# A two-layer decoder on one core: the last expert stage and the last norm in one stage, hidden rows made transposed

## The chip, the cores and the metric

The kernel runs on one core of one Trainium2 chip. The metric is the device time of one execution in microseconds (us), lower is better; the times before are the median of three runs. A profile comes from one further execution. The engines are TensorE (PE, with its weight loads as PEld), VectorE (DVE), ScalarE (ACT), GpSimd (POOL) and SyncE (SP). SyncE only issues DMAs here. ACTq, SPq and POOLq stand for what these engines' sequencers issue, DMAs above all.

## The reference, cut to what matters

A batch of 32 sequences of 128 tokens with 128 features passes six sublayers; each is followed by a residual add and a layer norm without gain. All is float32. The last two sublayers are a gated recurrence over the 128 positions (`_L1_xattn_ref`) and a switch layer, in which each token goes to one of 8 experts:

```python
logits = t @ switch_w + switch_b
route_prob = jax.nn.softmax(logits, axis=-1)
route_prob_max = jnp.max(route_prob, axis=-1)
routes = jnp.argmax(route_prob, axis=-1)
for e in range(8):
    h = jax.nn.gelu(t @ w1[e] + b1[e])      # w1: 128 x 512
    y = h @ w2[e] + b2[e]                   # w2: 512 x 128
    out = jnp.where((routes == e)[:, None], y, out)
out = out * route_prob_max[:, None]
...
x = _layernorm(x + _L1_ffn_ref(...))
```

## The kernel before

The program is a row of phases. Each is a `Phase`: its engines' programs are written out side by side and joined by semaphores, and at its end stands a barrier over all engines. `phase_encode` does the first layer's attention and cross attention and `phase_experts` (tag `m0`) its experts; `phase_decode` does the second layer's attention, `phase_recurrent` its recurrence, `phase_experts` (tag `m1`) the switch experts, and `phase_finish` the last residual and norm. In every phase the order of work on an engine is written out by hand as ticks: in each tick an engine takes tile n of one step, tile n-2 of another, and so on.

**`phase_recurrent` (L1759).** One tick is one position of the recurrence, for 32 sequences: VectorE multiplies gate and state (`gated`, L2002), TensorE adds the product to `drive` (L1879), ScalarE takes the tanh (L1946), and VectorE waits for it. Beside this chain, four positions make a line of 128 tokens: its output product, its norm (`x6`, the residual of the last sublayer; statistics L2008, GpSimd's power function L1859, scaling L1966) and its routing logits. Four lines make a quad, which VectorE routes at the ticks `quad_at(tick, 29)` to `(tick, 38)`: distance to the largest logit (`gap`), the chosen expert (`hot`), and the rows in the sorted table. GpSimd scatters the line's 128 rows into `scratch_sorted1` (L1850), a table with one region for each expert; SyncE stores the line to `scratch_x6` as well (L1832). `RING` is 12 line buffers. After the last line, VectorE builds the tables (`dve_table`, L427): which expert each of 40 tiles of 128 sorted rows belongs to, and where it begins. SyncE writes a tile of zeros behind each expert's rows (`sp_pads`, L418), ScalarE takes the exponential of all gaps (L1987), and VectorE makes the weights of it.

**`phase_experts` (L1184), tag `m1`.** 40 tiles, which is the most that can be needed; a tick is one tile. SyncE loads a tile of sorted rows (L1230). TensorE transposes it (L1255), ScalarE copies the transpose to SBUF (L1313), TensorE multiplies it with the expert's up weights, which are the moving operand, 512 columns (L1249). VectorE adds the up bias (L1290), ScalarE takes the Gelu (L1326), TensorE transposes the four blocks of 128 hidden columns (L1259), VectorE copies them to SBUF (L1296), TensorE multiplies them with the down weights (L1267), VectorE adds the down bias (L1301) and SyncE stores the tile to `scratch_expert_out1` (L1234). Up and down weights of all experts lie in SBUF, 2 MB each, loaded in `phase_decode` (L1477), and so do the biases, repeated in all partitions.

**`phase_finish` (L2091).** Eight turns of four lines, in a loop with two sets of buffers. SyncE loads four lines of `x6` (L2114), GpSimd gathers each token's expert row with an indirect DMA (L1350), VectorE multiplies with the weight and adds the residual (L2162), takes statistics (L214, L218), GpSimd takes the power function of the variances (L261), VectorE scales (L242) and ScalarE's queue stores the line (L2130).

Of the kernel before, what the change touches and what calls it, by code (L numbers as in the profile page):

```python
# [20 lines left out]
G = 4  # L21
# [11 lines left out]
TILES1 = TOKENS // P + EXPERTS  # L33

# [71 lines left out]
def dram_tile(d, n):  # L106
# [9 lines left out]
    ("a_w1", FF1), ("a_w2", FF1), ("mask_q", G), ("part_iota", 1), ("a_bq", 1), ("a_bk", 1), ("x_bq", 1),  # L116
# [301 lines left out]
def sp_pads(sp, c, t, sorted_rows):  # L418

    sp.wait_ge(t["free_ready"], 1)  # L420
    for e in range(EXPERTS):
        row = sp.value_load(t["free"][0:1, e:e + 1], min_val=0, max_val=EXPERTS * REGION - P)
        sp.dma_start(sorted_rows[bass.ds(row, P), :], c["zeros"][:]).then_inc(t["padded"], 16)
    sp.wait_ge(t["padded"], 16 * EXPERTS)

def dve_table(nc, dve, c, kept, t):  # L427
# [9 lines left out]
    def step(ins):  # L437
# [17 lines left out]
    step(nc.vector.tensor_scalar(tile[:], c["iota_tiles"][:, 0:tiles], last[:], None, ALU.min))  # L455
# [8 lines left out]
                                        op0=ALU.mult, op1=ALU.add))  # L464
    nc.vector.tensor_copy(kept["tile_expert"][:], expert[:])
# [79 lines left out]
def phase_encode(nc, c, d, scr, keep, experts0):  # L545

    with Phase(nc) as ctx:
# [47 lines left out]
        def _(sp):  # L595
# [22 lines left out]
            sp_pads(sp, c, table, scr["sorted0"])  # L618
# [545 lines left out]
def expert_buffers(nc, ctx, tag, down):  # L1164
    def sb(name, shape):
        return ctx.enter_context(nc.sbuf_tensor(name + tag, shape, F32))
    return dict(up=sb("up", [P, EXPERTS, FF1]), up_b=sb("up_b", [P, EXPERTS, FF1]),
                 down=sb("down", [P, EXPERTS, down, P]), down_b=sb("down_b", [P, EXPERTS, P]))

def load_experts(sp, keep, e, d, names, parts=(0, 1, 2, 3)):

    up, down, up_b, down_b = names
    for part in parts:
        tile, src = ((e["up"], d[up]), (e["down"], d[down]), (e["up_b"], d[up_b].partition_broadcast(P)),
                     (e["down_b"], d[down_b].partition_broadcast(P)))[part]
        sp.dma_start(tile[:], src).then_inc(keep["experts_loaded"], 16)
# [238 lines left out]
def phase_decode(nc, c, d, keep, scr, xT_all, experts1, recur):  # L1416
# [4 lines left out]
    with Phase(nc) as ctx:  # L1421
# [45 lines left out]
        def _(sp):  # L1467
# [291 lines left out]
def phase_recurrent(nc, c, scr, keep, e, xT_all):  # L1759
# [5 lines left out]
    with Phase(nc) as ctx:  # L1765
# [19 lines left out]
        x6, x6T = [sb(f"x6_{k}", [P, P]) for k in range(RING)], pair("x6T", [P, P])  # L1785
        stats, mv, ve, rstd, shift = ([sb(f"{n}{k}", [P, w]) for k in range(4)] for n, w in (
            ("stats", 6), ("mean_var", 2), ("var_eps", 1), ("rstd", 1), ("shift", 1)))
        raw, logits, gap = sb("raw", [P, SLOTS, EXPERTS]), sb("logits", [P, SLOTS, EXPERTS]), sb("gap", [P, TILES, EXPERTS])
# [5 lines left out]
        total = sb("total", [P, TILES])  # L1794
# [13 lines left out]
        gaps_ready, weighed = sem("gaps_ready"), sem("weighed")  # L1808
# [276 lines left out]

LINKS6 = 16

def phase_finish(nc, c, keep, scr, out):  # L2091
# [198 lines left out]
```

## Time and profile before

| | |
|---|---|
| median of 3 runs | 1457.57 us (1446.95 to 1458.02) |
| profiled execution | 1453.48 us, span of its trace 1451.7 us |
| busy share of the span | TensorE 83%, VectorE 74%, ScalarE 58%, GpSimd 37% |
| recurrent stage | up to about 1285 us |
| second expert stage | about 1285 to 1383 us |
| finish | about 1385 us to the end |

### The profile page before, as it was taken

To read this page: it belongs to the slowest core of one execution; us is meant where nothing else is said; L and a number is where in the kernel's file an instruction comes from. 1 tells how busy PE (TensorE), PEld (TensorE's weight loads), DVE (VectorE), ACT (ScalarE), POOL (GpSimd) and SP (SyncE) were. 2 spreads that over 40 slices of the span, in tenths; PEclk is the share of its full clock that TensorE was granted. 3 is DMA by queue.
4 is the path that set the end of the run, shared out by engine and by line. 5 is a ranking of instruction groups with operands and counts; after the bars stand their busy time and mean duration, and the time that the engine had idled before them with its cause. 6 is when DMAs were issued, how large, how long until landed. Compare 5 with 4: busy or idle time off the path is not lost. (4 is left out here: it accounts for less than half of the span.)

```text
span 1451.7 us, 31640 instructions
## 1 busy us (share of the span) xinstructions
PE 1207.3 (83%) x9948; PEld 806.1 (56%) x9948; DVE 1076.9 (74%) x3184; ACT 845.2 (58%) x2331; POOL 534.8 (37%) x798
## 2 busy tenths in 40 slices
PE   3889999999999999872999689999997899859900
PEld 2556666666666656541666355555554777637700
DVE  3578888888888888764788599999997466456644
ACT  2678878787878788641566256666665344333300
POOL 1233324344444444424000465655531146510065
PEclk9999999999999999985999799999999599779965
DMA  7100000000000000001222223130000001112133
GB/s 275 28 13 14 16 16 27 20 25 22 23 23 22 22 16 14 14 10 57 69 84 82 58 98 125 40 94 23 22 5 1 6 24 41 36 59 59 50 92 90
DMA packets 84815, 65.88 MB, mean 45 GB/s; under 512 B 11440, under 2 KB 79792, under 8 KB 83760
## 3 DMA queue, kind: packets, MB, share of 16 engines
q1 hardware_dynamic: 73856, 47.18, 10.5%
q0 software_dynamic: 6144, 12.60, 2.6%
q10 hardware_dynamic: 4656, 4.10, 0.9%
q8 instruction: 85, 1.39, 0.4%
q14 instruction: 74, 0.61, 0.1%
HBM read 40.76 MB, written 23.07 MB: 44 GB/s over the span
## 5 line engine op out<-in xcount | busy, mean ns | idle before, releaser
L693 PE MATMUL e_bank_turned<-c_matrices,e_probs 128*128 128x128 f32 x1024 | 165.0, 285 | 17.2 <-ACT e_probs_t L925 9.8
L925 ACT ACTIVATE e_probs_t<-e_bank_turned 128x512 f32<-128x512 f32 x256 | 154.8, 605 | 16.6 <-PE e_bank_turned L693 14.9
L629 POOL TENSOR_TENSOR e_rstd<-e_var_eps,c_minus_half 128x1 f32<-128x1 f32 x128 | 71.1, 576 | 250.6 <-DVE e_var_eps L961 250.3
L1047 DVE TENSOR_REDUCE e_neg_max<-e_bank_scores 128x4 f32<-128x512 f32 x160 | 109.6, 685 | 49.2 <-PE e_bank_scores L736 48.6
L693 PEld LDWEIGHTS e_bank_turned<-c_matrices,e_probs 128*128 128x128 f32 x1024 | 115.9, 144 | 40.8 <-issue 17.0
L703 PE MATMUL e_bank_mix<-e_probs_t,e_values 128*32 128x128 f32 x2048 | 111.5, 291 | 15.7 <-ACT e_probs_t L925 15.4
L884 ACT ACTIVATE e_probs<-e_scores,e_neg_max 128x128 f32<-128x128 f32 x384 | 123.3, 410 | 1.1 <-DVE e_neg_max L1083 1.1
L1249 PE MATMUL m_wide<-up,m_rowsT 128*128 x224 | 119.0, 614 | 0.5 <-ACT m_rowsT L1313 0.4
L1657 ACT ACTIVATE d_probs_t<-d_bank_turned 128x512 f32<-128x512 f32 x128 | 77.3, 604 | 62.7 <-PE d_bank_turned L1542 62.6
L1290 DVE TENSOR_TENSOR m_pre<-m_wide,up_b 128x512 f32<-128x512 f32 x112 | 77.3, 690 | 43.9 <-PE m_wide L1249 42.8
L879 ACT ACTIVATE e_probs<-e_scores 128x512 f32<-128x512 f32 x128 | 82.1, 641 | 42.1 <-DVE e_scores L1080 41.6
L632 POOL TENSOR_TENSOR e_k_by_place<-e_q_k_k,c_matrices 128x512 f32<-128x512 f32 x64 | 66.6, 1040 | 102.4 <-DVE e_q_k_k L1091 102.4
L1641 ACT ACTIVATE d_probs<-d_scores 128x512 f32<-128x512 f32 x128 | 80.8, 631 | 39.5 <-DVE d_scores L1680 39.5
L1542 PE MATMUL d_bank_turned<-c_matrices,d_probs 128*128 128x128 f32 x512 | 81.8, 283 | 21.4 <-ACT d_probs_t L1657 21.3
L1680 DVE TENSOR_TENSOR d_scores<-d_bank_scores,d_neg_max 128x512 f32<-128x512 f32 x128 | 88.5, 692 | 4.4
L1080 DVE TENSOR_TENSOR e_scores<-e_bank_scores,e_neg_max 128x512 f32<-128x512 f32 x128 | 88.3, 690 | 3.4
L1313 ACT ACTIVATE m_rowsT<-m_turned_rows 128x128 f32<-128x128 f32 x112 | 30.9, 276 | 100.3 <-PE m_turned_rows L1255 100.2
L1676 DVE TENSOR_REDUCE d_neg_max<-d_bank_scores 128x4 f32<-128x512 f32 x128 | 87.5, 683 | 2.3 <-PE d_bank_scores L1533 2.0
L1542 PEld LDWEIGHTS d_bank_turned<-c_matrices,d_probs 128*128 128x128 f32 x512 | 55.3, 141 | 57.2 <-issue 51.0
L1267 PE MATMUL m_sums<-down,m_hT 128*128 x608 | 86.5, 276 | 0.1
L1488 POOL DMA_INDIRECT d_first<-scratch_expert_out,keep_out_rows x32 | 32.1, 1003 | 138.2 <-POOLq L82 132.5
L1267 PEld LDWEIGHTS m_sums<-down,m_hT 128*128 128x128 f32 x608 | 76.7, 192 | 0.5 <-issue 0.3
(310 smaller groups left out, 3139.1 us busy)
## 6 DMA issues: line engine op xcount, KB each, us to landing
m_rows<-scratch_sorted SPq DMA_DIRECT2D x112, 64.0 KB, 1.7
scratch_expert_out<-m_y SPq DMA_DIRECT2D x112, 64.0 KB, 1.5
e_x_in<-in_x SPq DMA_DIRECT2D x32, 64.0 KB, 1.8
e_ctx_in<-in_ctx SPq DMA_DIRECT2D x32, 64.0 KB, 2.1
up<-in_m_wgv SPq DMA_DIRECT2D x1, 2048.0 KB, 7.6
up_b<-in_m_bgv SPq DMA_DIRECT2D x1, 2048.0 KB, 14.1
scratch_ctxT<-e_xT_ctxT SPq DMA_DIRECT2D x32, 64.0 KB, 1.6
scratch_x<-e_x SPq DMA_DIRECT2D x32, 64.0 KB, 1.7
```

The source lines that it names most:

```text
L693: last = nc.tensor.transpose(turned_bank[:, j * P:(j + 1) * P], pr[k % 3][:, j, :], c["ident"][:])
L703: last = nc.tensor.matmul(mix_bank[32 * j:32 * j + VC, g * P:(g + 1) * P], lhsT=va[att][n % 3][:, G * g + j, :], rhs=pt[k % 2][:, j * P:(j ...
L879: nc.scalar.activation(pr[k % 3][:], sc[k % 4][:], ACT.Exp).then_inc(probs_ready, 1)
L884: last = nc.scalar.activation(pr[k % 3][:, j, :], src[:, j, :], ACT.Exp, bias=nmax[k % 4][:, j:j + 1], scale=1.0)
L925: nc.scalar.activation(pt[k % 2][:], turned_bank[:], ACT.Copy).then_inc(probs_t_ready, 1)
L1047: nc.vector.tensor_reduce(nmax[k % 4][:], bank, AX.X, ALU.max, negate=True).then_inc(max_ready, 1)
L1080: nc.vector.tensor_tensor(sc[k % 4][:], bank, bcast(nmax[k % 4][:], P), ALU.add).then_inc(bank_read, 1)
L1249: nc.tensor.matmul(wide[n % SLOTS][:], lhsT=rowsT[n % SLOTS][:], rhs=tile_of(e["up"], experts[n]), start=True, stop=True).then_inc(up_done, 1)
L1267: last = nc.tensor.matmul(sums[n % 2][:, 0:P], lhsT=hT[n % SLOTS][:, k * P:(k + 1) * P], rhs=e["down"][:, bass.ds(experts[n], 1), k, :].re ...
L1542: last = nc.tensor.transpose(turned_bank[:, j * P:(j + 1) * P], pr[u % 3][:, j, :], c["ident"][:])
L1676: nc.vector.tensor_reduce(nmax[tick % 4][:], bank, AX.X, ALU.max, negate=True).then_inc(max_ready, 1)
L1680: nc.vector.tensor_tensor(sc[tick % 4][:], bank, bcast(nmax[tick % 4][:], P), ALU.add).then_inc(shifted, 1)
```

## The change

`phase_experts` for the second layer and `phase_finish` become one phase, `phase_last`.

- The sorted rows have 130 columns instead of 128: the token's 128 features, its weight, and its number as an integer. They carry the residual along, so `scratch_x6` and its stores and loads go, and so do `scratch_expert_out1`, the gathers and the second half of `dve_table`. Pad rows have a token number beyond the last.
- The weight is worked out in `phase_recurrent`, once for each quad. Exp becomes two sigmoids, `e^g = s(g) / s(-g)`, with two reciprocals, a product and a sum on VectorE. GpSimd copies the token numbers in.
- In the last phase the up weights are the stationary operand and the transposed rows the moving one, so the hidden layer comes out transposed: four products of 128 columns. ScalarE adds the bias, now a column, within the Gelu, block by block. The four transposes, the bias add and the copy on VectorE go.
- Up weights and up biases don't lie in SBUF any more. SyncE loads those of the tile's expert for every tile, 128 rows of 516 columns, into a ring of 4. It waits for a row buffer (ring of 12) until the tile twelve before has been scattered to the output.
- Behind the down product VectorE adds the bias, multiplies with the weight and adds the residual, takes the statistics, and GpSimd makes the inverse deviation for two tiles at a time. VectorE scales, and GpSimd scatters the 128 rows to the output by their token numbers with an indirect DMA that leaves out numbers beyond the last token.

```diff
 # load_experts in phase_decode
-                if b in (9, 12, 15, 18):
-                    load_experts(sp, keep, experts1, d, ("s_w1", "s_w2", "s_b1", "s_b2"), (b // 3 - 3,))
+                if b in (9, 15):
+                    load_experts(sp, keep, experts1, d, ("", "s_w2", "", "s_b2"), (1 if b == 9 else 3,))
 # phase_recurrent, sync
-            for n in range(TILES):
-                sp.wait_ge(x6_ready, n + 1)
-                sp.dma_start(dram_tile(scr["x6"], n), x6[n % RING][:]).then_inc(x6_saved[n % RING], 16)
-            sp_pads(sp, c, table, scr["sorted1"])
+            sp.wait_ge(pad_ready, 1)
+            sp.dma_start(scr["sorted1"][EXPERTS * REGION:EXPERTS * REGION + P, :], pad[:]).then_inc(spare_padded, 16)
+            sp_pads(sp, pad, table, scr["sorted1"])
 # phase_recurrent, gpsimd
+                pool.wait_ge(x6_ready, (i + 1) * SLOTS)
+                nc.gpsimd.tensor_copy(x6_rows[:, at_slot:at_slot + SLOTS, P + 1].bitcast(U32), tokens[:, i * SLOTS:(i + 1) * SLOTS])\
+                    .then_inc(tokens_ready, 1)
...
+                if n >= 7 and n % 4 == 3:
+                    name(n // 4 - 1)
...
+            name(TILES // SLOTS - 1)
             for n in range(TILES - 8, TILES):
                 scatter(n)
 # phase_recurrent, scalar
+                if (i := quad_at(tick, 31)) is not None:
+                    act.wait_ge(gaps_ready, i + 1)
...
+                    nc.scalar.activation(ex[:], gap[:], ACT.Sigmoid)
+                    nc.scalar.activation(rest[:], gap[:], ACT.Sigmoid, scale=-1.0).then_inc(ex_ready, 1)
...
-            nc.scalar.activation(gap[:], gap[:], ACT.Exp).then_inc(weighed, 1)
 # phase_recurrent, vector
+                if (i := quad_at(tick, 36)) is not None:
+                    at_slot = i * SLOTS % RING
+                    dve.wait_ge(ex_ready, i + 1)
+                    chain.wait(chain.mark(nc.vector.reciprocal(rest[:], rest[:])))
+                    chain.wait(chain.mark(nc.vector.tensor_tensor(ex[:], ex[:], rest[:], ALU.mult)))
+                    chain.wait(chain.mark(nc.vector.reduce_sum(total[:], ex[:], AX.X)))
+                    dve.wait_ge(x6_ready, (i + 1) * SLOTS)
+                    weighed = chain.mark(nc.vector.reciprocal(x6_rows[:, at_slot:at_slot + SLOTS, P], total[:]))
 # phase_last
+ROWS_AHEAD, ROWS_RING = 6, 12
+UPS = 4
+X7_RING = 6
+        TICKS = range(-2, tiles + 7)
+        # sync
+            for n in range(-ROWS_AHEAD, tiles):
+                k = n + ROWS_AHEAD
+                if k < tiles:
+                    if k % SLOTS == 0:
+                        at_rows = row_of(k // SLOTS)
+                    if k >= ROWS_RING:
+                        sp.wait_ge(scattered[(k - ROWS_RING) % X7_RING], 16 * ((k - ROWS_RING) // X7_RING + 1))
+                    sp.dma_start(rows[k % ROWS_RING][:], sorted_rows[bass.ds(at_rows[k % SLOTS], P), :])\
+                        .then_inc(rows_loaded[k % ROWS_RING], 16)
+                k = n + UPS
+                if 0 <= k < tiles:
+                    if k % SLOTS == 0:
+                        experts = expert_of(k // SLOTS)
+                    if k >= UPS:
+                        sp.wait_ge(hT_ready, k - UPS + 1)
+                    sp.dma_start(up[k % UPS][:], dram_tile(d["s_up"], experts[k % SLOTS])).then_inc(up_loaded[k % UPS], 16)
+        # gpsimd
+            for n in range(-2, tiles):
+                k = n // 2 + 1
+                if n % 2 == 0 and 2 * k < tiles:
+                    pool.wait_ge(mean_ready, 2 * k + 2)
+                    if k >= 2:
+                        pool.wait_ge(x7_ready, 2 * k - 2)
+                    nc.gpsimd.tensor_scalar_add(ve[k % 2][:], mv[k % 2][:, :, 1], EPS).then_inc(ve_ready, 1)
+                    pool.wait_ge(ve_ready, k + 1)
+                    nc.gpsimd.tensor_tensor(rstd[k % 2][:], ve[k % 2][:], c["minus_half"][:, 0:2], ALU.pow).then_inc(rstd_ready, 1)
+                if n >= 0:
+                    pool.wait_ge(x7_ready, n + 1)
+                    nc.gpsimd.indirect_dma_start(
+                        out=out_rows, in_=x7[n % X7_RING][:], in_offset=None, bounds_check=TOKENS - 1, oob_is_err=False,
+                        out_offset=bass.IndirectOffsetOnAxis(ap=rows[n % ROWS_RING][:, P + 1:ROW1].bitcast(U32), axis=0))\
+                        .then_inc(scattered[n % X7_RING], 16)
+        # tensor
+                if 0 <= (n := tick) < tiles:
+                    pe.wait_ge(rowsT_ready, n + 1)
+                    pe.wait_ge(up_loaded[n % UPS], 16 * (n // UPS + 1))
...
+                    for k in range(BLOCKS1):
+                        last = nc.tensor.matmul(hidden_bank[n % SLOTS][:, k * P:(k + 1) * P], lhsT=up[n % UPS][:, k * P:(k + 1) * P],
+                                                rhs=rowsT[n % 4][:], start=True, stop=True)
+                if 0 <= (n := tick + 2) < tiles:
+                    pe.wait_ge(rows_loaded[n % ROWS_RING], 16 * (n // ROWS_RING + 1))
...
+                    nc.tensor.transpose(turned_rows[n % 2][:, 0:P], rows[n % ROWS_RING][:, 0:P], c["ident"][:]).then_inc(rows_turned, 1)
+                if 0 <= (n := tick - 2) < tiles:
+                    pe.wait_ge(hT_ready, n + 1)
...
+                    for k in range(BLOCKS1):
+                        last = nc.tensor.matmul(
+                            sums[n % 2][:, 0:P], lhsT=hT[n % 4][:, k * P:(k + 1) * P],
+                            rhs=e["down"][:, bass.ds(experts[n % SLOTS], 1), k, :].rearrange("p o n -> p (o n)"),
+                            start=k == 0, stop=k == BLOCKS1 - 1)
+        # vector: n is the tick's tile less 2, 5 and 2
+                    nc.vector.tensor_tensor(y[n % 2][:], sums[n % 2][:, 0:P], tile_of(e["down_b"], experts[n % SLOTS]), ALU.add)\
+                        .then_inc(y_ready, 1)
...
+                    dve.wait_ge(rstd_ready, n // 2 + 1)
+                    if n >= X7_RING:
+                        dve.wait_ge(scattered[n % X7_RING], 16 * (n // X7_RING))
+                    nc.vector.tensor_scalar(x7[n % X7_RING][:], sub[n % 4][:], mv[n // 2 % 2][:, n % 2, 0:1], rstd[n // 2 % 2][:, n % 2:n % 2 + 1],
+                                            ALU.subtract, ALU.mult).then_inc(x7_ready, 1)
...
+                    nc.vector.scalar_tensor_tensor(out=sub[n % 4][:], in0=y[n % 2][:], scalar=rows[n % ROWS_RING][:, P:P + 1],
+                                                   in1=rows[n % ROWS_RING][:, 0:P], op0=ALU.mult, op1=ALU.add).then_inc(joined, 1)
+                    nc.vector.bn_stats(stats[n % 2][:], sub[n % 4][:]).then_inc(stats_ready, 1)
+                    nc.vector.bn_aggr(mv[n // 2 % 2][:, n % 2, :], stats[n % 2][:]).then_inc(mean_ready, 1)
+        # scalar: row copy of tile tick + 2, Gelu of tile tick
+                    for k in range(BLOCKS1):
+                        last = nc.scalar.activation(hT[n % 4][:, k * P:(k + 1) * P], hidden_bank[n % SLOTS][:, k * P:(k + 1) * P],
+                                                    ACT.Gelu_apprx_tanh, bias=up[n % UPS][:, FF1 + k:FF1 + k + 1])
```

## Rows read from the trace of the kernel before

**Rows 1.** Chain; stretches: PE, PEld, DVE, ACT, POOL busy, clock, DMA, GB/s.

```profile
POOL 2%; issue 2%; POOLq 0%; DVE 0%; DVEq 0%
...
1297.00:1375.00 78.00, 78.00 (x511) 60.05 (x510) 53.61 (x102) 30.84 (x68) 0.00 (x0) 1.00 0.20 56
...
1386.00:1446.00 60.00, 0.00 (x0) 0.00 (x0) 29.10 (x136) 0.00 (x0) 41.30 (x54) 0.51 0.36 101
...
5.00:9.00 4.00, 0.00 (x0) 0.00 (x0) 0.00 (x0) 0.00 (x0) 0.00 (x0) 1.00 1.04 428
```

**Rows 2.** Timeline, second expert stage and last store: start us, us, engine, line, instruction.

```profile
1285.12 0.94 SPq L1230 DMA_DIRECT2D m_rows<-scratch_sorted  x2
...
1288.18 2.07 PE L1249 MATMUL m_wide<-up,m_rowsT 128*128 x2 [0.17 <-issue]
...
1331.70 0.97 PEld L1267 LDWEIGHTS m_sums<-down,m_hT 128*128 128x128 f32 x8
...
1332.60 0.30 PEld L1249 LDWEIGHTS m_wide<-up,m_rowsT 128*128 128x128 f32 x2
...
1333.01 0.29 DVE L1301 TENSOR_TENSOR m_y<-m_sums,down_b 128x128 f32<-128x128 f32 x1 [0.15 <-PE m_sums L1267]
...
1333.57 0.27 PE L1255 MATMUL m_turned_rows<-c_matrices,m_rows 128*128 128x128 f32 x1
...
1334.00 0.97 PEld L1267 LDWEIGHTS m_sums<-down,m_hT 128*128 128x128 f32 x8
...
1445.35 2.98 ACTq L2130 DMA_DIRECT2D out_x<-f_x_odd  x4
```

**Rows 3.** ScalarE: timeline of four biased exponentials; groups by line, second expert stage.

```profile
399.78 1.28 ACT L884 ACTIVATE e_probs<-e_scores,e_neg_max 128x128 f32<-128x128 f32 x4
...
L1313 ACT ACTIVATE m_rowsT<-m_turned_rows 128x128 f32<-128x128 f32 x34 | 9.4, 277 | 32.1 <-PE m_turned_rows L1255 32.1
```

**Rows 4.** GpSimd: timeline in the recurrent stage; groups by line in the finish.

```profile
1200.17 1.08 POOL L1850 DMA_INDIRECT scratch_sorted<-n_x,n_row_u  x1 [0.16 <-issue]
...
1201.55 0.96 POOL L1850 DMA_INDIRECT scratch_sorted<-n_x,n_row_u  x1 [0.30 <-issue]
...
1202.59 0.23 POOL L1858 TENSOR_SCALAR n_var_eps<-n_mean_var 128x1 f32<-128x1 f32 x1
...
1202.90 0.57 POOL L1859 TENSOR_TENSOR n_rstd<-n_var_eps,c_minus_half 128x1 f32<-128x1 f32 x1
...
L1350 POOL DMA_INDIRECT f_g_y<-scratch_expert_out,f_g_rows x32 | 30.9, 966 | 13.7 <-issue 7.3 <-POOL f_g_rows L1345 6.4
...
L261 POOL TENSOR_TENSOR f_rstd<-f_var_eps,c_minus_half 128x4 f32<-128x4 f32 x8 | 8.4, 1047 | 4.0 <-DVE f_var_eps L220 3.8
```

**Rows 5.** VectorE, groups by line in the finish: busy us, mean ns.

```profile
L2162 DVE SCALAR_TENSOR_TENSOR f_sub_odd<-f_g_y,f_g_weights,f_x_odd 128x128 f32<-128x128 f32 x16 | 4.6, 347 | 0.1
...
L214 DVE BATCH_NORM_STATS2 f_stats<-f_sub_odd 128x6 f32<-128x128 f32 x16 | 3.5, 279 | 0.0
...
L218 DVE BATCH_NORM_AGGREGATE f_mean_var<-f_stats 128x2 f32<-128x6 f32 x32 | 3.8, 161 | 0.2
```

**Rows 6.** DMA issues by line: count, KB each, median us from issue to landing.

```profile
m_rows<-scratch_sorted SPq DMA_DIRECT2D x39, 64.0 KB, 1.8
...
f_x_odd<-scratch_x SPq DMA_DIRECT2D x16, 64.0 KB, 3.3
...
scratch_sorted<-n_x,n_row_u POOLq DMA_INDIRECT x32, 2.3
...
up<-in_s_w SPq DMA_DIRECT2D x1, 2048.0 KB, 9.0
```

**Rows 7.** VectorE, recurrent stage: timeline of a step, one group by line.

```profile
1206.65 0.42 DVE L2046 SCALAR_TENSOR_TENSOR n_blend<-n_gates,n_inp 128x256 f32<-128x256 f32 x1
...
1207.46 0.19 DVE L2002 TENSOR_TENSOR n_gated<-n_gates,n_states 128x32 f32<-128x32 f32 x1 [0.39 <-ACT n_states L1946]
...
L2083 DVE RECIPROCAL keep_weights<-n_total 128x32 f32<-128x32 f32 x1 | 0.4, 353 | 0.0
```

More of the change, by code:

```diff
@@ L453, in dve_table @@
     step(nc.vector.tensor_scalar_add(last[:], end[:, EXPERTS - 1:EXPERTS], -1.0))
-    step(nc.vector.tensor_scalar(tile[:], c["iota_tiles"][:, 0:tiles], last[:], None, ALU.min))
+    if returned:
+        step(nc.vector.tensor_scalar(tile[:], c["iota_tiles"][:, 0:tiles], last[:], None, ALU.min))
+    else:
+        step(nc.vector.tensor_copy(tile[:], c["iota_tiles"][:, 0:tiles]))
     step(nc.vector.tensor_tensor(past[:], bcast(tile[:], EXPERTS), repeat(end[:], tiles), ALU.is_ge))
@@ L464, in dve_table @@
                                         op0=ALU.mult, op1=ALU.add))
+    if not returned:
+        nc.vector.tensor_scalar(kept["tile_expert"][:], expert[:], float(EXPERTS - 1), None, ALU.min)
+        step(nc.vector.tensor_scalar(kept["tile_row"][:], row[:], float(EXPERTS * REGION), None, ALU.min))
+        return
     nc.vector.tensor_copy(kept["tile_expert"][:], expert[:])
@@ L1174, in load_experts @@
     for part in parts:
[L1175 to L1177 removed]
+        tile = e[("up", "down", "up_b", "down_b")[part]]
+        src = d[(up, down, up_b, down_b)[part]]
+        sp.dma_start(tile[:], src if part < 2 else src.partition_broadcast(P)).then_inc(keep["experts_loaded"], 16)
 AHEAD = 8
@@ L2070, in _ @@
                     rows = kept["rows"][:, i * SLOTS:(i + 1) * SLOTS, 0]
+                    chain.wait(weighed)
                     chain.wait(put_step)
@@ L2108, in _ @@
         @block.sync
         def _(sp):
-            give_leads(sp, ctx)
-            def load(i, h):
-                for s in range(SLOTS):
-                    sp.dma_start(x6[h][s][:], dram_tile(scr["x6"], i * SLOTS + s)).then_inc(x6_loaded[h][s], 16)
-            load(0, 0)
-            load(1, 1)
-            with sp.Fori(0, TURNS // 2 - 1) as pair:
-                for h in range(2):
-                    sp.wait_ge(joined, pair * (2 * SLOTS) + (h + 1) * SLOTS)
-                    load(pair * 2 + (h + 2), h)
+            row_of, expert_of = loader(sp, "row", "tile_row", EXPERTS * REGION), loader(sp, "in", "tile_expert", EXPERTS - 1)
@@ new lines, in _ @@
+        @block.gpsimd
+        def _(pool):
+            for n in range(-2, tiles):
[13 more added lines that the diff above has]
+                        .then_inc(scattered[n % X7_RING], 16)
+            for s in range(X7_RING):
+                pool.wait_ge(scattered[s], 16 * len(range(s, tiles, X7_RING)))
```

200 lines of the change are left out of this document (111 added, 89 removed).

## The prediction

> **What bounds the kernel now.** I first read the page's chain of waits. It ends in the last stage, with GpSimd's gathers and its power function in alternation: GpSimd and its issue gaps have 2% of the span each, no other engine any [rows 1]. Busy time by stretch then splits what follows the recurrent stage in two [rows 1]. From 1297 to 1375 us, in the second expert stage, TensorE is busy all the time at granted clock 1.00 while DMA is busy 0.20 of the time. From 1386 to 1446 us, in the finish, TensorE and ScalarE do nothing, GpSimd is busy 41.3 of 60 us and DMA moves 101 GB/s. The two follow each other, with a barrier between.
>
> The timeline gives one tile of the expert stage [rows 2]. The eight weight loads of the four down products begin at 1331.70, the up product's at 1332.60, the row transpose and the four transposes of the hidden layer run from 1333.57, and the next tile's down begins at 1334.00. So a tile is 2.30 us: down 0.90, up 0.87 (two passes of 512 columns), five transposes 0.54 (0.11 each). A pass over 128 columns is thus 0.11 us, whether its weights change or not. The first up product starts at 1288.18, 3.06 us after the first row load is issued at 1285.12. The last output store is issued at 1445.35, four of them in 2.98 us; the span ends at 1451.7. I take about 2 us from the last landing to the end (estimate: 3.4 us lie between the last issue's end and the span's end, less a landing of about 1.5).
>
> **The change, part by part.** The finish stage disappears, so everything after the last tile's down product is now one tile's drain. What counts is the new pitch per tile, and where the last tile stands.
>
> *TensorE.* Up becomes four products with the weights stationary and 128 columns moving: 8 passes, 0.90 us. The hidden layer comes out transposed, so four of five transposes go. Row transpose 0.11, down 0.90. Sum 17 x 0.11 and the group rounding: 1.91 us per tile instead of 2.30.
>
> *ScalarE.* Four Gelus of 128x128 with a bias column cost at most what four exponentials with a bias column do, 1.28 us, plus the row copy of 0.28 [rows 3]: 1.56 us, under 1.91 and hidden.
>
> *VectorE.* Down bias 0.29 [rows 2], residual 0.35, statistics 0.28, aggregate 0.16 [rows 5], final scaling about 0.34 (as the residual): 1.42 us and some gaps, hidden as throughput. Its latency counts below.
>
> *GpSimd.* A pair of indirect DMAs takes 1.38 + 1.04 us from issue to the next instruction, with 0.16 of idle before; an add to its power function is 0.31; the power function is 0.57 for one column and 1.05 for four [rows 4], so I take 0.73 for two, plus 0.08 [rows 4]. A pair of tiles: 0.16 + 2.42 + 0.31 + 0.81 = 3.70, or 1.85 per tile. It fits under 1.91 by a hair. The bounds check that drops pad rows has no row of its own. I take nothing; above, the slowest of these issues is 1.38 against 1.04, which would make 2.0 per tile.
>
> The Trainium skill has a rule that speaks against this (SBUF — State Buffer, "Who interferes with whom" and the box on DVE blocking DMA): a VectorE tensor_scalar or copy from SBUF to SBUF takes the port pair that it shares with GpSimd, and a DMA issued from GpSimd can't write its descriptors meanwhile. In this trace such scalings and gathers already stand side by side in the finish: the indirect DMAs there have a mean of 0.97 us [rows 4]. By the rows the sum stays at 1.85; by the rule it is a rival, below.
>
> *The loop that I take for the bound.* SyncE issues, for tile n, the row load of tile n+6 and behind it the 258 KB of up weights of tile n+4. The row load has to wait until the scatter of tile n-6 has landed, since the 12 row buffers hold residual, weight and index until then. So the up load of tile m+10 hangs on the scatter of tile m. From the end of TensorE's tick m+5, in which down of tile m+3 is done: 0.41 until VectorE starts [rows 2]; 1.32 to the aggregate (0.29 + 0.35 + 0.28 + 0.16, gaps, and the scaling in between); 0.09 + 0.31 + 0.81 + 0.16 = 1.37 until the scatter of m is issued (the pair's norm stands ahead of it) [rows 4]; 2.3 to land [rows 6]; 0.05 + 0.61 for SyncE's two issues (two of them, 0.33 each, take 0.94: [rows 2]); the up load. Its landing: 64 KB take 1.8 and 2048 KB take 9.0 [rows 6], so 0.0036 us per KB and 2.5 for 258 KB. Sum 8.6 us; with tick m+5 itself 10.5 from its start to that of tick m+10, and 11.0 every other time, since SyncE then reads a table between its two issues (0.5, estimate). Only even tiles have this position (an odd tile's scatter comes one tick sooner and 1.38 later, which gives 1.98 a tick), so TensorE waits at even ticks' starts, which lengthens the odd ticks. In five ticks from m+5 there are two at 1.91 and three long ones: (10.75 - 3.82) / 3 = 2.3, mean 2.1. Nothing in this is hidden: TensorE waits at the up product.
> Bounds: if scatters and loads land as fast as the quickest (1.5 instead of 2.3, and no 0.7 for size), the loop is under 1.91 and TensorE binds. If they land as in the finish (3.3 for a 64 KB load [rows 6], so 4.0 for the weights, and the scatter 0.5 later), the sum is 10.5 and the tick 2.4.
> Traffic as such fits: 258 + 65 + 64 KB per 2.1 us is 190 GB/s, and the constants came in at 428 GB/s [rows 1].
>
> *Start.* The up weights of tile 0 are SyncE's fourth load and need a second table read: issued about 2.3 us after the first, landed 2.5 later, so the first up product starts at +4.8 instead of +3.06. The first one lasts 2.07 us now [rows 2], where a later one takes 0.87: a low clock. Two such ticks of 2.1 and one of 0.9 that has no down product yet: tick 3 at +9.9.
>
> *Recurrent stage.* Each quad of lines gets, on VectorE, a reciprocal (0.35), two steps of 0.19 and a small reciprocal, about 0.95 us with gaps, in the tick that has already the blend of 0.42. The blend leaves 0.39 idle until the next gated product [rows 7]; the rest, about 0.45, delays the state chain, in the 6 quads inside the recurrence: 2.7 us. Below: nothing, if TensorE's queue binds there; above: 0.95 x 8 = 7.6. The two sigmoids (ScalarE, some 0.3) fit in the idle 0.5 behind the gates. The last quad's steps put off the table by 0.25. The token copy and pads at the head, below 0.3; and the spare pad's DMA is early. The names' copy on GpSimd is 0.18 per quad, hidden in its idle time; it shifts the last scatters by 0.8, under the eight pad DMAs that end the stage either way. The 32 stores of the residual go from SyncE's queue, and nothing waited for them. In all +3.0.
> *Decode and constants.* Two loads of 2 MB fewer and 16 KB more constants: both stood beside work that didn't wait for them; nothing.
>
> *Drain.* After the last up product starts: down of tile 39 starts +2.8 and is seen +4.0, VectorE's aggregate +5.2, the norm of the last pair +6.4, then four scatters in a row (GpSimd takes this norm before tile 36's scatter), the last issued +10.4, landed +12.7, end +14.7.
>
> **Sum.** 1285.1 + 3.0 = 1288.1; tick 3 at 1298.0; to tick 10 at 1.91: 1311.4; 29 ticks at 2.1: 1372.3; drain: 1387.0. The profiled execution took 1453.48 for a span of 1451.7, so 1388.8 us, 64.7 less. It lies 4 us under the median of 1457.57, inside the runs' spread (1446.95 to 1458.02). I say 1389.
>
> **Rivals.**
> 1. The loop is faster than I think and TensorE binds at 1.91: 29 x 0.19 = 5.5 less, 1383. For it: the landings' quickest. Chance 0.15.
> 2. GpSimd binds. By the port rule each tile's scaling (0.34) adds to it: 2.2 per tile, 1389 + 36 x 0.1 = 1393; if the residual's two inputs block its reads too (0.35), 2.55 and 1405. This is the skill's rule above as a mechanism of this kernel. Against it: 0.97 in the finish. Chance 0.15.
> 3. Landings stretch under 190 GB/s, tick 2.4: 29 x 0.3 = 9, 1398. For it: 3.3 us in the finish at 101 GB/s [rows 1, 6]. Chance 0.17.
> 4. The weights' traffic binds and the kernel gets slower. 387 KB per tile at the finish's 101 GB/s would be 3.8 us a tile, 1389 + 36 x 1.7 = 1450; it becomes slower than before beyond 3.9 us a tile, at under 98 GB/s. At 90 GB/s it is 4.3: 1468. Against it: the finish had DMA busy 0.36 only, its rate was set by GpSimd, and the first microseconds show 428. Chance 0.03.
>
> **How the numbers follow.** My forecast, tick 2.0 to 2.2: chance 0.5. It and rivals 1 to 3 lie in 1383 to 1405; the recurrence's bounds add -3 and +5, and the runs' spread before was 11 us. Range 1372 to 1404. A run of this kernel can tell a difference of about 1% from none. Faster by over 1%: 0.96, all but rival 4; within 1% 0.01; slower 0.03.
>
> **What would show it.** TensorE's tick in the last stage (start to start of up products) at 2.05 to 2.15, with its idle time ahead of the up product and released by the weights' DMA. GpSimd's idle time there, small but not nil; if nil, rival 2. The scatter's landing near 2.3 and the weights' near 2.5. In the recurrent stage a gated product about 0.45 late once per 16 steps. I'm wrong if TensorE waits for something other than the weights' load, or if the rise in the recurrent stage is above 8 us.

## The result and the profile after

The changed kernel takes 1406.36 us (median of 4 runs, 1401.51 to 1408.77) against 1455.8 for the kernel before on the same chip: a ratio of 0.9667, 95% interval 0.9618 to 0.9716. It is faster by 49 us. I had forecast 1389 and a range that ended at 1404, so the direction was right and the size was not.

In the page of the profiled execution (1406.4 us) TensorE has the largest share of the chain of waits that ended last, 6% of the span. Below it stand the stretches of the last stage; their columns are those of [rows 1].

```profile
span 1404.5 us, 31524 instructions
...
PE 6%; issue 1%; POOL 0%; DMA 0%; SPq 0%; DVE 0%; DVEq 0%; POOLq 0%
```

```profile
1297.00:1310.00 13.00, 13.00 (x106) 13.00 (x106) 5.57 (x21) 10.39 (x37) 2.14 (x5) 0.89 0.65 175
1310.00:1350.00 40.00, 32.85 (x280) 31.47 (x278) 22.16 (x87) 22.13 (x85) 26.17 (x36) 1.00 0.57 157
1350.00:1385.00 35.00, 31.65 (x250) 31.36 (x251) 17.73 (x69) 18.16 (x70) 20.44 (x27) 0.90 0.58 158
1386.00:1398.00 12.00, 3.26 (x29) 3.07 (x28) 6.05 (x23) 1.89 (x8) 9.79 (x13) 0.75 0.06 18
```

The finish of [rows 1] is gone. But where TensorE was busy without a gap at 2.30 us a tile, it is now busy 32.85 of 40 us, and GpSimd only 26.17. So neither binds: something between them does. The starts of two up products give the pitch: tick 10 starts at 1315.76 and tick 39 at 1385.37, 69.61 us for 29 ticks, 2.40 a tick. A tick that waits for nothing is 1.895.

SyncE's waits from 1300 to 1380 say for what (engine and line, the releaser, us in total, times, longest):

```profile
SPq L2172 <- DMA out_x<-f_x,f_rows: 23.5, 15, 3.1
```

L2172 is the row load, and it waits for the output scatter. One round of the loop in the timeline, for the scatter of tile 14 and the up product of tile 24 (start us, us):

```profile
1337.85 0.97 PEld L2228 LDWEIGHTS f_sums<-down,f_hT 128*128 128x128 f32 x8
...
1340.61 0.22 POOL L2190 TENSOR_SCALAR f_var_eps<-f_mean_var 128x2 f32<-128x2 f32 x1 [0.92 <-DVE f_mean_var L2262]
1340.91 0.72 POOL L2192 TENSOR_TENSOR f_rstd<-f_var_eps,c_minus_half 128x2 f32<-128x2 f32 x1
1341.82 1.07 POOL L2195 DMA_INDIRECT out_x<-f_x,f_rows  x1 [0.19 <-issue]
...
1345.74 0.33 SPq L2172 DMA_DIRECT2D f_rows<-scratch_sorted  x1
1347.15 0.27 SPq L2180 DMA_DIRECT2D f_up<-in_s_up  x1
...
1350.03 0.97 PEld L2213 LDWEIGHTS f_hidden<-f_rowsT,f_up 128*128 128x128 f32 x8 [2.29 <-issue]
```

The down product of tick 19 ends near 1338.75. It is 3.07 us to the scatter's issue (forecast 3.10), then 3.92 until the next row load can be issued (forecast 2.35), 1.41 to the weights' issue behind it (forecast 1.1), and 2.88 to the product (forecast 2.5). The loop is the one of the forecast; its transfers land later. The profile names no releaser for TensorE's wait ("issue"). The row copy of tile 24 had ended at 1345.46, TensorE was free at about 1347.7, and SyncE had issued the weights at 1347.15, so the weights were the last to come; that this loop sets the pitch is shown by the row buffers below.

### The profile page after: what moved, and what is told of

It reads as the page before. It is cut to its first block and busy times, and to the rows that moved or that the text cites. A ratio compares the mean times of both kernels' runs of the same rounds, so it can differ in the third digit from the quotient of the medians.

```text
span 1404.5 us, 31524 instructions
## 1 busy us (share of the span) xinstructions
PE 1194.4 (85%) x10028; PEld 809.5 (58%) x10028; DVE 1038.4 (74%) x3150; ACT 863.6 (61%) x2465; POOL 555.0 (40%) x830
## 3 DMA queue, kind: packets, MB, share of 16 engines
q8 instruction: 85, 1.39, 0.4%
## 5 line engine op out<-in xcount | busy, mean ns | idle before, releaser
L687 POOL DMA_INDIRECT scratch_sorted<-e_x,e_row_u x64 | 65.2, 1019 | 31.8 <-DVE e_row_u L1042 16.3
L711 PEld LDWEIGHTS e_bank_mix<-e_probs_t,e_values 128*32 128x32 f32 x2048 | 40.9, 109 | 63.3 <-issue 34.2
L1257 PE MATMUL m_wide<-up,m_rowsT 128*128 x144 | 76.0, 611 | 0.4 <-ACT m_rowsT L1321 0.4
L1965 ACT ACTIVATE n_states<-n_bank_drive 128x32 f32<-128x32 f32 x128 | 25.3, 198 | 70.8 <-PE n_bank_drive L1898 69.0
L1057 DVE TENSOR_TENSOR e_scores<-e_bank_scores,c_bias 128x512 f32<-128x512 f32 x96 | 65.5, 683 | 0.0
```

Of the source, the lines that this page charges most:

```text
L711: last = nc.tensor.matmul(mix_bank[32 * j:32 * j + VC, g * P:(g + 1) * P], lhsT=va[att][n % 3][:, G * g + j, :], rhs=pt[k % 2][:, j * P:(j ...
```

## The experiments

Each time is a median; the ratio is to the kernel before on the same chip, with its 95% interval. The first eight comparisons ran on one chip, on which the kernel before took 1457.1 and 1456.9 us, and the last four on a faster one (1452.0). Ticks are the mean from tick 10 to tick 39.

**Three edits to the loop, and half of the change alone.** 24 row buffers:

```diff
-ROWS_AHEAD, ROWS_RING = 6, 12
+ROWS_AHEAD, ROWS_RING = 6, 24
```

> 24 row buffers instead of 12 in the last stage, so a row load waits for the scatter of 18 tiles back instead of 6 back; all else as in the changed kernel, weights' traffic included. Theory A (the loop binds: SyncE holds the next weights behind a row load that waits for a scatter): TensorE's waits at even ticks go, the tick falls from 2.40 to 1.91 us, 29 x 0.49 = 14 us less, 1392. Rival B (the weights' own transfers are too slow under 190 GB/s, whatever SyncE waits for): the tick stays at 2.3 to 2.4, 1403 to 1407. Rival C (GpSimd is next, just above TensorE): tick 1.97 to 2.05, 1394 to 1397, with GpSimd without idle time.

Measured: 1392.98 us, ratio 0.9557 (0.954 to 0.9575). The tick is 1.908. The last stage is now TensorE's alone, at a higher traffic than in the changed kernel:

```profile
1316.00:1372.00 56.00, 55.84 (x500) 55.67 (x500) 37.94 (x148) 37.84 (x147) 45.02 (x59) 1.00 0.70 197
```

Theory A holds, rivals B and C fall: the transfers carry 197 GB/s without a wait, and GpSimd is busy 45.0 of 56 us, 1.53 a tile.

The thin load, which keeps every wait and takes the bytes away:

```diff
-sp.dma_start(up[k % UPS][:], dram_tile(d["s_up"], ...))
+if k >= UPS:
+    sp.dma_start(up[k % UPS][:, FF1:], dram_tile(d["s_up"], ...)[:, FF1:])
+else: ...  # as before
```

> From the fifth tile on the weights' load brings only the four bias columns (2 KB instead of 258 KB), so the products use old weights; the order and the waits of SyncE's queue are those of the changed kernel, with 12 row buffers. Theory A with landings stretched by the traffic: scatter issued to next row load issued 2.5 us instead of 3.7, the thin load lands in 2.1 to 2.3 instead of 2.9, so the loop is 9.4 instead of 11.3 and the tick 2.1 to 2.2: 1398 to 1401. If the traffic does not stretch anything, 3.7 stays, only the size goes (0.6 us of 11.3) and the tick is 2.3: 1404. Rival B: 1.91 and 1392.

Measured: 1402.26 us, 0.9626 (0.9605 to 0.9646); tick 2.18, of the forecast 2.1 to 2.2. The total is 1 us above it, since this execution came to the last stage 2.6 us later than the changed kernel's. Without the weights' bytes TensorE's tick is still 0.29 above the 1.895 that waits for nothing, against 0.50 with them: with 12 row buffers the loop costs time even at this traffic, and the traffic adds to it.

The weights' loads on ScalarE's queue:

```diff
 for tick in TICKS:          # ScalarE
+    if 1 <= tick and (k := tick + UPS - 1) < tiles:
+        act.wait_ge(hT_ready, tick)
+        act.dma_start(up[k % UPS][:], dram_tile(d["s_up"], ...))
```

> The weights' loads are issued from ScalarE's queue instead of SyncE's (same waits on the hidden layer, same 12 row buffers, same traffic), so they no longer stand behind the row loads' wait for a scatter. Theory A: tick 1.91 and the first weights 1.5 us earlier: 1406.4 - 14.2 - 1.5 = 1391. If the issue costs ScalarE 0.5 us a tile it still fits under 1.91 (1.42 + 0.5). Rival B: tick 2.3 to 2.4, only the start's 1.5 us: 1405. Rival C: 1393 to 1396.

Measured: 1403.73 us, 0.9633 (0.9614 to 0.9652); tick 2.23. A miss for theory A as I had put it. TensorE's waits from 1290 to 1400 give one reason:

```profile
PE f_turned_rows L2213 <- DMA f_rows<-scratch_sorted: 23.6, 4, 19.2
...
PEld f_turned_rows L2213 <- DMA f_rows<-scratch_sorted: 5.0, 3, 2.5
```

(19.2 of the first is the start.) TensorE now waits at the row transpose, for the row load: the loop has a second branch, which I had not counted. The row load of tile m+12 itself hangs on scatter m, and its transpose comes two ticks ahead of its product.

Only the merged finish, with the hidden layer in the old form and resident up weights:

```diff
-for k in range(BLOCKS1):
-    nc.tensor.matmul(hidden[:, k*P:(k+1)*P], lhsT=up[n % UPS][:, k*P:(k+1)*P], rhs=rowsT)
+nc.tensor.matmul(hidden, lhsT=rowsT, rhs=tile_of(e["up"], expert))
+...  # bias on VectorE, one Gelu of 128x512, four transposes two ticks later
```

> Only the other half of the change: residual, weight, last norm and scatter in the last stage as in the changed kernel, but the up product, its bias, the Gelu and the four transposes in the old form, with the up weights and bias resident (loaded in the decode stage as before). TensorE 2.30 to 2.33 us a tile and no weights' traffic. Theory A: tick 2.33 with no waits, first up product 1.8 us earlier than in the changed kernel, drain 2 us longer by the extra tick of pipeline: 1402 to 1406, so the transposed form brings nothing of the 49 us as it stands. Rival D (VectorE, 0.69 + 1.42 and gaps, is over 2.3 now): tick 2.5, 1409 to 1412. If the transposed form did pay as forecast by TensorE's 0.39 us a tile: 1417 or more.

Measured: 1413.48 us, 0.9698 (0.9683 to 0.9714). The tick is 2.43: 2.30 free, and waits for the row loads here too, though at 52 GB/s (waits from 1320 to 1392):

```profile
PEld f_turned_rows L2215 <- DMA f_rows<-scratch_sorted: 10.1, 12, 1.7
```

So with 12 buffers the merged finish alone gives a ratio of 0.970, and the transposed form adds little to it: the whole change has 0.967, and 0.966 in its second comparison. Of TensorE's 0.39 us a tile, 15 us for 39 tiles, some 5 arrive; the interval of the first comparison, which ends at 0.9716, does not tell them from none. What the transposed form is worth without the waits was not measured: the old form was not run with more row buffers. The total is 8 us above my 1402 to 1406. In the trace its first row load is issued at 1297.0, 7.2 later than the changed kernel's; 4.6 of that is the clock at the head of the recurrent stage, of which more below.

**The loop again, the traffic doubled, and the recurrent stage.** The double load:

```diff
-sp.dma_start(up[k % UPS][:], dram_tile(...))
+sp.dma_start(up2[k % UPS][:], dram_tile(...).unsqueeze(1).to_broadcast([P, 2, FF1 + BLOCKS1]))
```

> The weights' load brings its 258 KB twice (516 KB a tile), into a buffer twice as wide; 12 row buffers, and all waits as in the changed kernel. Loop theory with landings stretched by traffic: the weights' landing grows from 2.9 to at least 3.5 (516 KB at the 428 GB/s of the constants is 1.2 us, against 0.6), and scatter to next row load from 3.7 to 4.5 or more: loop 11.3 to 12.7 or more, tick 2.65 to 3.0, 29 x 0.25 to 29 x 0.6 = 7 to 17 us more, 1414 to 1424, plus 1 to 2 at the start. Rival (size and traffic matter little): within 3 us of 1406.

Measured: 1430.01 us, 0.9798 (0.9768 to 0.9829); tick 2.99, the upper end of what I expected, and a total above it. With the changed kernel and the thin load it makes a series in which only the weights' bytes differ. These are medians from the traces, over the even tiles m = 0 to 26; the last but one column only where TensorE waited. The traffic is that of the stretches from 1317 to 1380, 1310 to 1385, 1310 to 1383 and 1325 to 1411 us. The second trace of the changed kernel is the one described under "the changed kernel again".

| kernel | GB/s, about ticks 10 to 39 | scatter issued to next row load issued, us | weights issued to product, us | tick, us |
|---|---|---|---|---|
| thin load | 59 | 2.76 | 1.73 | 2.18 |
| changed kernel | 157 | 3.69 | 2.90 | 2.40 |
| changed kernel, second trace | 154 | 3.38 | 2.86 | 2.53 |
| double load | 217 | 4.64 | 4.17 | 2.99 |

The scatter is the same 64 KB in all of them. Its landing is stretched by other transfers in flight. In the double load the 4.64 is not all landing: the scatter of tile 4 had landed after 2.33 us and the next row load was issued after 6.57, so something else held SyncE there. The two kernels below that leave the last stage as it is give 3.47 and 3.50 us and ticks of 2.36 and 2.47, so one and the same last stage spreads over 0.3 us from scatter to row load and over 0.17 in the tick; the thin and the double load lie outside that. The Trainium skill (DMA: Bandwidth & Descriptors, "Queues, rings and completion order") says that each DMA engine takes turns between the queues that it has work for, a packet at a time. The series agrees with that, 0.93 us later with one load of weights a tile (0.62 in the second trace) and 1.88 with two; that it is this mechanism was not tested.

14 row buffers instead of 12:

```diff
-ROWS_AHEAD, ROWS_RING = 6, 12
+ROWS_AHEAD, ROWS_RING = 6, 14
```

> 14 row buffers instead of 12, nothing else. By the loop as measured (11.3 us from the end of tick m+5 to the start of the up product that hangs on scatter m, 13.2 from that tick's start), the up product that hangs on it is now that of tile m+12, seven ticks on: 13.2 / 7 = 1.89, just under TensorE's 1.895. So nearly all of the gain of 24 buffers comes with two: tick 1.90 to 2.0, 1393 to 1396. If instead the gain of 24 came from having more row loads in flight or from spreading the traffic, 14 buffers bring a sixth of it: tick 2.3, 1404.

Measured: 1386.37 us, 0.9537 (0.9513 to 0.9561). Tick 1.909, as with 24. SyncE still waits for scatters (its waits from 1300 to 1380), and nothing comes of it (the stretch below):

```profile
SPq L2172 <- DMA out_x<-f_x,f_rows: 16.0, 16, 2.0
```

```profile
1312.00:1368.00 56.00, 55.84 (x501) 55.68 (x500) 37.74 (x147) 38.58 (x148) 43.94 (x59) 1.00 0.70 198
```

The median from scatter to next row load is 3.70 here. It is as long as in the changed kernel, but has two ticks more to hide in. What cost the time was the distance of the loop, not the traffic as such. Against the changed kernel on the same chip (below) it is 17.1 us less, and 29 ticks of 0.62 less are 18.0. About 4 of these 18 are ticks that the changed kernel's second trace ran at a low granted clock (0.50 to 0.69), each time after a wait of 3.9 to 4.5 us; such waits are gone here.

Six up buffers:

```diff
-UPS = 4
+UPS = 6
```

> Six up buffers instead of four, each weights' load issued right behind the row load of the same tile, 12 row buffers. The weights' branch of the loop gets two ticks more, as with 14 row buffers; the branch through the rows (scatter m, row load m+12, its transpose two ticks before its up product) stays: 3.07 + 3.7 + 3 = 9.8 us from the end of tick m+5, against 8.5 until TensorE comes to that transpose. So waits at the row transpose, tick 2.1 to 2.25 as with the loads on ScalarE's queue (2.21): 1397 to 1402, the start 1.2 us earlier included. If the rows' branch does not bind (what ScalarE lost there was its own issue time): 1.91 and 1391.

Measured: 1389.69 us, 0.9577 (0.9554 to 0.96); tick 2.09. With the second branch as the bound I had said 2.1 to 2.25, without it 1.91. From 1307 to 1368 TensorE waits for rows, and as long ahead of down products:

```profile
PEld f_turned_rows L2220 <- DMA f_rows<-scratch_sorted: 2.5, 3, 1.0
PEld f_sums L2228 <- issue: 2.3, 5, 0.9
```

The longest of the second kind stand where the queue of TensorE reads the table of experts, once in four tiles: the read ends at 1350.43 and the down product starts at 1351.01. So of the 5.7 us above TensorE's own pace (29 ticks of 0.195) the rows' branch is shown for 2.5.

The total is below the 1397 to 1402 that I gave, but this chip is faster by 5 us (1452.0 for the kernel before). Against the changed kernel on the same chip it is 13.7 us less, and 29 ticks of 0.44 less are 12.8. The loads on ScalarE's queue had 2.23 with the same rows' branch. The 0.14 between them is not shown to be ScalarE's: there TensorE waited 6.0 us for row loads over the 29 ticks instead of 2.5, and its ticks 32 and 33 lost 1.7 us at a granted clock of 0.88 and 0.63. Two traces of one program differ as much (2.40 and 2.53).

The weights' VectorE steps spread over steps 33, 35, 36 and 38 of a quad:

```diff
-if (i := quad_at(tick, 36)) is not None: reciprocal; product; sum; reciprocal
+33: reciprocal   35: product   36: sum   38: reciprocal
```

> Only the recurrent stage is edited: the four VectorE steps of a quad's weights (0.34 + 0.21 + 0.19 + 0.18 us) no longer stand in one step beside the blend, but one each in steps 33, 35, 36 and 38 of the quad, which have 0.34 to 0.50 us idle. My theory of that stage: the six gated products that come 1.38 us after the one before instead of 0.96 go back to 0.96 or so: 6 x 0.42 = 2.5 us less, first row load and end both earlier, 1404 against 1406.4. Rival: another step of the same quad takes the delay over (VectorE's queue is in order, and the reciprocal fits by 0.05 only): under 1 us. The time at which TensorE's clock rises in that stage moves from kernel to kernel by up to 17 us, which is worth up to 5 us, so the pitches of the trace decide, not the total alone.

Measured: 1409.55 us, 0.9674 (0.9653 to 0.9695): nothing won in the total, yet the delay is gone. The timeline of VectorE, first the changed kernel with all four steps in one place:

```profile
1207.30 0.42 DVE L2071 SCALAR_TENSOR_TENSOR n_blend<-n_gates,n_inp 128x256 f32<-128x256 f32 x1
1207.63 0.34 DVE L2091 RECIPROCAL n_rest<-n_rest 128x32 f32<-128x32 f32 x1
1208.01 0.21 DVE L2092 TENSOR_TENSOR n_ex<-n_ex,n_rest 128x32 f32<-128x32 f32 x1
1208.25 0.19 DVE L2093 TENSOR_REDUCE n_total<-n_ex 128x4 f32<-128x32 f32 x1
1208.47 0.18 DVE L2095 RECIPROCAL n_x<-n_total 128x4 f32<-128x4 f32 x1
1208.57 0.16 DVE L2024 TENSOR_TENSOR n_gated<-n_gates,n_states 128x32 f32<-128x32 f32 x1
```

then the spread form:

```profile
1222.61 0.42 DVE L2071 SCALAR_TENSOR_TENSOR n_blend<-n_gates,n_inp 128x256 f32<-128x256 f32 x1
1222.94 0.18 DVE L2096 TENSOR_REDUCE n_total<-n_ex 128x4 f32<-128x32 f32 x1
1223.42 0.19 DVE L2024 TENSOR_TENSOR n_gated<-n_gates,n_states 128x32 f32<-128x32 f32 x1 [0.30 <-ACT n_states L1965]
```

Without an idle time in brackets the gated product came late; with one, VectorE was ready and waited for the state. From gated product 31 to 112, all at full clock, the time is 76.7 us before the change, 79.5 with it, 77.5 spread: 2.0 of 2.9 us come back. The 0.8 left are two steps of 1.34 us, near 1201 and 1233, which every trace with the change has; the kernel before has one of 1.26. Why is open. The total doesn't show it, for two reasons. The clock's low level took 36.2 us for the first 31 steps in this execution, 31.7 in the changed kernel's; and its last stage had a tick of 2.47.

The pads' places with one register load:

```diff
-for e in range(EXPERTS):
-    row = sp.value_load(t["free"][0:1, e:e + 1], ...)
+sp.load(regs, t["free"][0:1, 0:EXPERTS])
+for reg in regs: row = sp.snap(reg)...
```

> The eight pad rows' places are read into SyncE's registers with one load instead of one load ahead of each of the eight DMAs, in both stages that write pads. The eight issues now take 9.4 us from the first to the first row load at the end of the recurrent stage (1.18 each). If the register reads are most of that: about 0.5 a DMA, 4.0 + 0.9 instead of 9.4, so 4 us less there, and up to 4 at the end of the first stage if nothing else ends later: 1398 to 1402. Rival: the DMAs' own issue and landing are the 1.18, or GpSimd's last scatters end as late (its last one is issued at 1280.7 and lands at about 1283): 1 us or less in the first, 1405.

Measured: 1405.35 us, 0.9639 (0.9615 to 0.9662), the same as the changed kernel as far as this can tell. From the first pad's issue to the first row load it is 10.2 us instead of the 11.2 and 12.5 in the changed kernel's two traces. GpSimd's last scatter, issued 6.2 us ahead of the first row load, is the likely next one to end late; that was not tried alone.

**The changed kernel again**, unedited:

> The changed kernel once more, unedited, to see what two profiled executions of one program differ by. The last stage's tick: 2.40 in the first trace; if the loop sets it, 2.3 to 2.45 again. The recurrent stage: its slow-clock head was 9 steps of 1.15 to 1.28 us here and 13 to 26 in the kernels with edits elsewhere. If the length of that head is chance, it comes out different now; if the program fixes it, 9 again. Total 1404 to 1410.

Measured: 1403.43 us, 0.9659 (0.9635 to 0.9682). The tick is 2.53 in this trace, above the 2.45 that I allowed. The first gated product comes at 1135.0 instead of 1139.3, and the first 31 steps take 33.3 us instead of 31.7. The first row load is issued at 1284.4 instead of 1289.8. So two executions of the same program are 5.4 us apart when the last stage is reached.

**Combinations.** All four edits at first, with the loads on ScalarE's queue:

> 24 row buffers, the weights' loads from ScalarE's queue, the weights' VectorE steps spread, and the pads' places read at once. Theory: 1393.0 (24 buffers alone) less 1.0 (first up product 3.8 us after the first row load instead of 4.8) less 2.5 (spread) less 4 (pads): 1385.5; if pads and spread bring nothing: 1392. Tick 1.91 in the last stage.

Measured: 1394.58 us, 0.9561 (0.9541 to 0.9581), no better than 24 buffers alone. Its tick is 2.03, with 24 buffers on SyncE's queue alone 1.908. The two longest waits, 1.05 and 1.25 us, stand ahead of up products whose row copies had ended 1.6 and 1.9 us before, so they are waits for weights. From ScalarE's queue the weights are issued 3.4 us ahead of their product (median of ticks 10 to 39), from SyncE's with 24 buffers 4.3. With six up buffers on SyncE's queue instead:

> 24 row buffers, six up buffers with the loads on SyncE's queue, the weights' VectorE steps spread, the pads' places read at once. Theory: tick 1.91; from 24 buffers alone (1393.0) less 1.2 (first weights issued behind the first row load) less 2.5 (spread) less 2.5 (pads: 10.2 instead of 12.5 to 13.9 from the first pad to the first row load, seen alone): 1387. If the clock's slow head in the recurrent stage takes the spread's gain again: 1390.

Measured: 1382.23 us, 0.9514 (0.9495 to 0.9533), and a tick of 1.892, which is TensorE's own:

```profile
1307.00:1362.00 55.00, 55.00 (x496) 55.00 (x495) 37.29 (x145) 37.99 (x146) 43.59 (x58) 1.00 0.71 192
```

It beats both kernels, the changed one by some 21 us (1403.43 on the same chip). How much of that is due to anything beyond the row buffers stays open: the interval overlaps that of 14 row buffers alone.

## Why the forecast was right in its mechanism and wrong in its size

| point | forecast, us | changed kernel, us | added there |
|---|---|---|---|
| first row load issued | 1288.1 | 1289.8 | 1.7 |
| tick 3 | 1298.0 | 1301.0 | 1.3 |
| tick 10 | 1311.4 | 1315.8 | 1.4 |
| tick 39 | 1372.3 | 1385.4 | 8.7 |
| end of the span | 1387.0 | 1404.5 | 4.4 |

**The step that failed is the loop's sum of 8.6 us**, in two of its terms. "2.3 to land" and SyncE's 0.05 were 3.69, and the weights' 2.5 were 2.90. The rest held: 3.07 for 3.10, and 0.85 between SyncE's two issues for 0.61 and a table read of 0.5 every other time. Sum 10.5. Put into the forecast's own formula that gives (10.5 + 1.9 - 3.8) / 3 = 2.87 for the long ticks and 2.38 in the mean; 2.40 was measured. That this is so close is partly luck, since the clock is in the 2.40 (next paragraph) and the waits are uneven: from none to 2.3 us in this trace, up to 4.5 in the second. For the thin load the same formula gives 2.0 from its medians, and 2.18 was measured. I took the scatter's 2.3 from the recurrent stage, where DMA moved 34 GB/s (1165 to 1265 us) [rows 6], and used it in a stage for which I had worked out 190. Rival 3 said what happened, with the tick of 2.4 itself, and I gave it 0.17. Its sum was 10.5 too, but it put most of the addition on the weights (4.0) and 0.5 on the scatter, and measured it is 0.4 on the weights and 1.3 on the scatter. The row that it stood on, 3.3 us for a load under 101 GB/s [rows 1, 6], was the nearest in traffic, and by the rule of taking the nearest row it should have been the forecast. That traffic stretches the landings is shown by the thin and the double load.

The loop alone would not have left the range: 1388.8 and 8.7 are 1397.5. The other 8.8 us of the table are the time of the first row load, the start, the loop's first wait ahead of tick 10 and the drain, below.

Some of the 2.40 is the clock. After the waits of 2.3 us ahead of ticks 24 and 32 the granted clock is low (0.67 to 0.71 in the mean of a tick), and ticks 24, 25, 32 and 33 lose 0.7 to 0.9 us each, 3.2 in all or 0.11 a tick. Not every such wait has this behind it: in the thin load's trace a wait of 2.8 us ahead of tick 20 was followed by ticks at full clock.

**Even tiles only**: right. The waits stand at the starts of even ticks. **TensorE's tick of 1.91**: right (1.895). **The up branch alone**: incomplete. With the other branch taken away (six up buffers) there are still waits for rows, and the tick is 2.09; about half of what it has above 1.895 is these waits.

**GpSimd** came out as costed: 1.07 and 0.97 for the two scatters, 0.22 and 0.72 for the pair's norm, against 1.38 and 1.04 with their gaps, 0.31 and 0.81. The bounds check costs nothing that shows. Rival 2 falls. A VectorE scaling of 0.34 runs at the same time as 22 of the 40 scatters. These take 1.08 us (first of a pair) and 0.97 (second), the others 1.06 and 0.97. By the port rule of the Trainium skill (SBUF — State Buffer, "Who interferes with whom") they could have grown; no row here shows that. Rival 1, a loop under TensorE's pace, was wrong for this kernel and right for 14 buffers.

**Ticks 3 to 10** have the loop's first wait, 1.4 us ahead of tick 10, which I had put behind it. **The start** lost 1.3 us, but not ahead of the first up product, which came 4.85 us after the first row load (forecast 4.8). Ticks 0 and 1 took 1.87 and 1.92 us, at the low clock, for 2.1 each. Tick 2 took 2.61 for 0.9: I had said that it has no down product, but it has that of tile 0, and part of it still ran at the low clock (0.71 in its mean):

```profile
1294.63 1.78 PEld L2213 LDWEIGHTS f_hidden<-f_rowsT,f_up 128*128 128x128 f32 x8 [2.28 <-issue]
...
1300.14 0.97 PEld L2228 LDWEIGHTS f_sums<-down,f_hT 128*128 128x128 f32 x8
...
1301.03 0.97 PEld L2213 LDWEIGHTS f_hidden<-f_rowsT,f_up 128*128 128x128 f32 x8
```

**The drain** took 19.2 us from tick 39's start, not 14.7, and 19.2 in the second trace:

```profile
1386.37 2.89 PE L2228 MATMUL f_sums<-down,f_hT 128*128 x24
...
1390.26 1.06 POOL L2195 DMA_INDIRECT out_x<-f_x,f_rows  x1
1391.63 0.97 POOL L2195 DMA_INDIRECT out_x<-f_x,f_rows  x1 [0.30 <-DVE f_x L2251]
1392.61 0.25 POOL L2190 TENSOR_SCALAR f_var_eps<-f_mean_var 128x2 f32<-128x2 f32 x1
1392.95 0.72 POOL L2192 TENSOR_TENSOR f_rstd<-f_var_eps,c_minus_half 128x2 f32<-128x2 f32 x1
1393.86 1.13 POOL L2195 DMA_INDIRECT out_x<-f_x,f_rows  x1 [0.19 <-issue]
...
1397.84 0.97 POOL L2195 DMA_INDIRECT out_x<-f_x,f_rows  x1 [0.31 <-issue]
```

VectorE's aggregate of tile 39 starts at +6.7, not the +5.2 by which I had it done, since VectorE still works off tiles 36 to 38. GpSimd, which I had taken as free for the last norm then, is busy with the scatters of tiles 34 and 35 until +7.2. So the last scatter is issued at +12.5 instead of +10.4. The end comes 6.7 us after it instead of 4.3: 2.1 until it has landed (forecast 2.3) and 4.6 from there to the end, for which I had estimated 2 from the finish's last stores [rows 2]. What these 4.6 us are is open.

**The recurrent stage**: the mechanism was right. The quads' steps cost 0.4 each, and the spread form takes that away. The first row load came 4.7 us later than before the change in this trace, but 0.7 earlier in the second trace of the same program. What goes beyond the 2.9 of the quads is within what two executions differ by.

## What to carry to other kernels

Count, for each buffer ring, how many ticks lie between the event that frees a buffer and the product that needs its next content, on every path that hangs on that event: here two buffers more were worth 17 us, and no engine's busy time said so. Take a transfer's landing from a row with the traffic that the changed stage will have, not from the same transfer in a quiet stage, and expect single waits well beyond what medians give. An issue queue that holds a load behind another load's wait passes that wait on.

## What the runs showed that I had not expected

The recurrent stage begins with TensorE at its low level, 1.2 GHz (granted clock 0.50 over the first eight steps of the changed kernel, 1.00 from the tenth): gated products 1.14 to 1.39 us apart, against 0.92 to 0.99 afterwards. When the clock rises varies from execution to execution, also of one program: the first 31 steps took 30.7 to 36.3 us over 14 traces, 31.7 and 33.3 in the two of the changed kernel. Differences of a few us between kernels are not to be read as their edits' work without the trace.

Under 197 GB/s the 258 KB loads of weights don't slow TensorE at all as long as nothing waits for a landing (tick 1.908). With the loop of 12 row buffers the tick is 0.50 us longer than TensorE's own at 157 GB/s, and still 0.29 longer at 59.

In both traces with the loads on ScalarE's queue TensorE's tick was longer than with the same buffers on SyncE's, by 0.13 and 0.14 us, though ScalarE was busy only 0.6 to 0.7 of the time. With 24 buffers the weights were issued later ahead of their product, as told above; with 12 the cause is open.
